# Attention 1: row loads over 48 data partitions, key rows of ones written once, products for maxima over 48 rows

## What is computed

```python
q = jnp.einsum('bld,dhe->blhe', x, Wq)
k = jnp.einsum('bld,dhe->blhe', x, Wk)
v = jnp.einsum('bld,dhe->blhe', x, Wv)
a = jnp.einsum('bqhd,bkhd->bhqk', q, k) / Dh ** 0.5
a = jnp.where(mask, a, NEG_INF)
a = jax.nn.softmax(a, axis=-1)
o = jnp.einsum('bhqk,bkhd->bqhd', a, v)
return jnp.einsum('blhe,hed->bld', o, Wout)
```

## Time and profile before

| | |
|---|---|
| median of 3 runs | 1116.33 us (1116.32 to 1117.96) |
| the profiled execution | 1120.27 us, its span 1118.5 us |
| attention 1's matmuls | from 476.8 us to about 821 us of the span |
| PE busy | 921.9 us (82%) |
| DVE busy | 781.9 us (70%) |
| ACT, POOL busy | 517.0 us (46%), 465.7 us (42%) |
| DMA queue 1 | 36189 packets, 45.41 MB, 13.5% of the 16 engines' time |
| granted clock of PE, mean of the span | 0.922 |

### The profile page before, as it was taken

The page is one execution under the profiler, slowest core; times in us unless marked ns, Lnnn a source line. Parts: engine busy times, 40 slices in busy tenths (PEclk is TensorE's granted clock), DMA queues, the critical chain, the costliest instruction groups (busy, mean ns, idle before and its releaser), DMA issues. The chain is left out here.

```text
span 1118.5 us, 18158 instructions
## 1 busy us (share of the span) xinstructions
PE 921.9 (82%) x6169; PEld 549.5 (49%) x6169; DVE 781.9 (70%) x1507; ACT 517.0 (46%) x755; POOL 465.7 (42%) x629
## 2 busy tenths in 40 slices
PE   6899999994476666457999888978839999999997
PEld 2445555552354444333444443434326776677765
DVE  6777777775688999367778786868545666666642
ACT  3666666785123334324767665756713122232221
POOL 3112222224345556612555564535434335453344
PEclk9999999998668889767999999989968999999999
DMA  9000000000000000343333332310000000000000
GB/s 287 18 10 10 9 9 9 9 0 20 9 20 9 9 26 10 86 123 104 98 91 90 95 101 82 94 71 5 12 1 11 20 7 12 19 19 19 9 1 19
DMA packets 36254, 46.25 MB, mean 41 GB/s; under 512 B 4134, under 2 KB 27174, under 8 KB 36190
## 3 DMA queue, kind: packets, MB, share of 16 engines
q1 hardware_dynamic: 36189, 45.41, 13.5%
HBM read 22.00 MB, written 15.27 MB: 33 GB/s over the span
## 5 line engine op out<-in xcount | busy, mean ns | idle before, releaser
L1553 ACT ACTIVATE PT<-PS 128x1024 f32<-128x1024 f32 x160 | 162.9, 1022 | 87.1 <-PE PS L1333 87.1
L1609 POOL TENSOR_SCALAR_AFFINE_SELECT PT<-PT 128x256 f32<-128x256 f32 (+1 forms) x224 | 95.0, 439 | 147.6 <-ACT PT L1553 146.5
L1948 POOL TENSOR_TENSOR PRE_sb<-PRE_sb,VA 128x512 f32<-128x512 f32 x64 | 82.2, 1284 | 146.8 <-DVE PRE_sb L1996 146.7
L1922 ACT ACTIVATE sg_d<-PS 128x512 f32<-128x512 f32 x64 | 38.2, 597 | 183.8 <-PE PS L1070 183.7
L1647 DVE TENSOR_REDUCE negm<-PS 128x2 f32<-128x1024 f32 x64 | 78.0, 1225 | 44.1 <-PE PS L1322 42.6
L356 ACT ACTIVATE E<-PS,m 128x512 f32<-128x512 f32 x128 | 86.2, 684 | 40.3 <-PE PS L281 25.5
L1996 DVE TENSOR_TENSOR PRE_sb<-sg_d,PS 128x512 f32<-128x512 f32 x64 | 43.5, 687 | 82.6 <-ACT sg_d L1922 81.3
L1348 PE MATMUL PS<-PT,VA 128*32 128x512 f32 (+3 forms) x1024 | 92.7, 459 | 3.3 <-POOL PT L1609 3.3
L1318 PE MATMUL PS<-kS,qS 51*128 51x384 bf16 (+3 forms) x512 | 75.9, 319 | 22.0 <-DVE spread L1750 8.6
L469 DVE TENSOR_SCALAR E<-E 128x512 f32<-128x512 f32 x128 | 68.6, 536 | 33.5 <-ACT E L356 29.7
L387 POOL TENSOR_SCALAR Qs<-Qs 128x1024 f32<-128x1024 f32 x32 | 35.0, 1096 | 116.2 <-ACT Qs L344 116.2
(11 more groups left out here) (269 smaller groups left out, 2130.1 us busy)
## 6 DMA issues: line engine op xcount, KB each, us to landing
qS<-qk_rows SPq DMA_DIRECT2D x32, 204.0 KB
kS<-qk_rows SPq DMA_DIRECT2D x32, 204.0 KB
qk_rows<-parts SPq DMA_DIRECT2D x32, 192.0 KB, 2.8
xs_sb<-XN_sb SPq DMA_DIRECT2D x23, 256.0 KB, 2.3
qk_rows<-parts SPq DMA_DIRECT2D x32, 128.0 KB, 2.8
X_sb<-in_x_dram SPq DMA_DIRECT2D x8, 256.0 KB, 6.8
gs<-PRE_sb SPq DMA_DIRECT2D x8, 256.0 KB, 2.3
qk_rows<-parts SPq DMA_DIRECT2D x32, 64.0 KB, 2.5
```

The costliest lines, as they stand in the source:

```text
L1553: nc.scalar.activation(PT[:, quad % 2, u, :], PS[:, b:b + 2, :].rearrange("p b n -> p (b n)"), ACT.Exp).then_inc(exp_ready, 1)
L1609: nc.gpsimd.affine_select(out=v, in_=v, pattern=[[0, 4 if u == 4 else 2], [1, P]], compare_op=ALU.is_ge, fill=0.0, base=0, channel_multipl ...
L1948: nc.gpsimd.tensor_tensor(acts[:, s, f, :], acts[:, s, f, :], W[:, slot, s, :], ALU.mult).then_inc(weighted, 1)
```

## The change

`qk_rows` has 48 rows in place of 51, and the row loads cover 48 partitions in place of 51. The ones of k's rows 48 to 50 no longer come with every load: `ones` is written into `kS`, for both slots and both `par`, by four DMAs in feed-forward 0 in place of the eight stores of `fixed` into DRAM. One memset on POOL goes. The products for maxima read 48 rows, the scores 51 as before.

```diff
-        self.fixed = sb("fixed", [3, 2, S], BF16)
+        self.ones = sb("ones", [3, S], BF16)
...
-        self.qk_rows = nc.dram_tensor("qk_rows", [2, 2, 2, 51, NPAIR * S], BF16, kind="Internal").ap()
+        self.qk_rows = nc.dram_tensor("qk_rows", [2, 2, 2, 6 * DH, NPAIR * S], BF16, kind="Internal").ap()
...
-            own, heads = slice(64 * par, 64 * par + 51), slice(4 * h, 4 * h + 4)
+            own, heads = slice(64 * par, 64 * par + 6 * DH), slice(4 * h, 4 * h + 4)
...
-            sp.wait_ge(cleared, 4)
+            sp.wait_ge(cleared, 3)
             for slot in range(2):
-                for m in range(2):
-                    for par in range(2):
-                        sp.dma_start(pr.qk_rows[slot, m, par, 48:51, :].rearrange("r (a s) -> r a s", a=NPAIR),
-                                     pr.fixed[:, m, :].unsqueeze(1).broadcast_to([3, NPAIR, S])).then_inc(fixed_out, 16)
+                for par in range(2):
+                    sp.dma_start(pr.kS[64 * par + 48:64 * par + 51, slot, :, :],
+                                 pr.ones[:, :].unsqueeze(1).broadcast_to([3, NPAIR, S])).then_inc(fixed_out, 16)
...
-            sp.wait_ge(fixed_out, 16 * 8)
+            sp.wait_ge(fixed_out, 16 * 4)
...
-            nc.gpsimd.memset(pr.fixed[:, 0, :], 0.0).then_inc(cleared, 1)
-            nc.gpsimd.memset(pr.fixed[:, 1, :], 1.0).then_inc(cleared, 1)
+            nc.gpsimd.memset(pr.ones[:, :], 1.0).then_inc(cleared, 1)
...
-            pool.wait_ge(cleared, 4)
+            pool.wait_ge(cleared, 3)
...
-            def operands(slot, quad, j):
-                own = slice(64 * (j % 2), 64 * (j % 2) + 51)
+            def operands(slot, quad, j, rows):
+                own = slice(64 * (j % 2), 64 * (j % 2) + rows)
...
-                        q, key = operands(slot, quad, j)
+                        q, key = operands(slot, quad, j, 48)
...
-                    q, key = operands(slot, quad, j)
+                    q, key = operands(slot, quad, j, 51)
```

## The result

The changed kernel takes 1089.64 us (median of 4 runs, 1087.02 to 1091.99) against 1116.32 us before (1116.18 to 1117.96): ratio 0.9742, 95% interval 0.9705 to 0.9778. The profiled execution took 1091.99 us, with a span of 1090.3.

A forecast was written before the change was run, and what follows sets the result against it. The prediction took PE to bound attention 1, held up by waits behind row loads of 51 partitions on three DMA engines. It summed -14.5 - 7.2 - 6 = -27.7 us off 1116.3, giving 1089 us, range 1082 to 1101.

The forecast's parts named there:

- Three engines with 51 partitions, sixteen with 48: Row loads in attention 1: DMA engines used are the largest number up to 16 dividing the partitions, 3 then 16.
- The loads' length: Four row loads ahead of an exchange of maxima: 4.5 us in place of 10.6.
- -14.5 us for the waits for the maxima: Attention 1: all seven waits of PE's scores matmuls for the load of the maxima go, 14.5 us.
- -7.2 us at the start: Start of attention 1: PE's wait for the staging of `xs`, issued behind eight row loads, goes, 7.2 us.
- -6 us for the clock: Attention 1: PE's time lost at the lower clock behind long stalls goes, 6 us, bounds 0 and -8.
- three stalls: Clock means from 530, 680 and 740 us: 12.2 us at the lower level behind stalls, half of it lost.
- Nothing given back: Attention 1 without the stalls: PE sets its own pace, so 0 us is given back, with 3 us as bound.
- DVE does not take over: Rival: PE's waits for DVE in attention 1 grow as its slack shrinks, 1099 or 1104 us; chance 0.08.
- Small edits: One POOL memset less, four DMAs for eight at feed-forward 0's end, matmuls over 48 rows: zero each.
- The issue of a row load: On SP: 0.30 us could become 0.61, sending the store of the maxima up to 1.2 us later, within 3 us slack.
- The lower end of the range, 1082 us: Whole kernel: the time with the clock at its bound and the first sequence faster too.
- The rivals that kept the loads slow: Row loads on as few engines: 1111 to 1116 us, chance 0.06; also costlier for SP to issue: 1124 us, chance 0.04.

The follow-up runs named there:

- the experiment at the start alone: Kernel before, with only the eight row loads of sequence 0 cut into 48 and 3 partitions, later loads keeping 51; 1111.51 us, ratio 0.9932.
- The stall that was put back: Kernel after, with only the row loads of half 0 of the last sequence cut into 17, 17 and 14 partitions; 1096.91 us, ratio 0.9806.
- the kernel with 48 and 3 partitions: Kernel before, with each row load cut into two DMAs of 48 and 3 partitions, fixed rows still loaded; 1087.94 us, ratio 0.9739.

## Why the prediction was right

The forecast was 1089 us, and 1089.64 was measured. By its steps:

- **Three engines with 51 partitions, sixteen with 48.** Right. The shares with 51, 52, 54, 57 and 17 partitions (0.19, 0.79, 0.57, 0.21, 0.06) and with 48 (full) are those of 3, 13, 9, 3, 1 and 16 engines, each the largest number up to 16 that divides the partitions. The Trainium skill states this rule ("DMA: Bandwidth & Descriptors", "Why a DMA increments its semaphore by 16 and not by 1"). These shares agree with it.
- **The loads' length.** I took 4.5 us for four loads, from the 175 GB/s of stores of 64 partitions; they took 4.8 us, at 167 GB/s from first packet to last. The estimate of 1.9 us came of the Trainium skill's rule for the engines (the same section) and of a rate that I let grow with them. The rule gives the engines, not the rate, and the rate did not grow so.
- **-14.5 us for the waits for the maxima.** Right: seven waits gone. But the working expected the store behind the loads still, with 3 to 8 us for the exchange; it takes 1.4 to 2.9. What I had not seen, and read from SP's timelines, is that the old exchange itself kept SP from issuing the next stores and loads in time. With a short one, the loads go out 7.5 us ahead of the store, and the slack is larger than I worked out.
- **-7.2 us at the start.** Right by PE's row at 479.24 and by the medians of the experiment at the start alone (-7.6 us, 4 to 11); that experiment's profile shows only 4.0 us of it at the end of attention 1, since its next stall grew.
- **-6 us for the clock.** The size came out, in part by luck: PE's busy time fell by 6.91 us for the same matmuls, but this is a gain of 9.03 us up to the last 54 matmul instructions and a loss of 2.13 in these. The rows before and after, split there:

```profile
476.77:810.57 333.80, 282.88 (x3451) 140.49 (x3453) 250.72 (x462) 204.45 (x247) 154.25 (x317) 0.92 0.28 81
810.57:829.43 18.86, 6.59 (x54) 3.55 (x54) 6.31 (x22) 2.69 (x5) 6.98 (x18) 0.74 0.01 1
```

```profile
475.08:779.48 304.40, 273.85 (x3451) 136.84 (x3453) 252.83 (x462) 204.42 (x247) 155.20 (x317) 0.96 0.37 84
779.48:800.49 21.01, 8.72 (x54) 4.53 (x54) 6.33 (x22) 2.69 (x5) 7.01 (x18) 0.60 0.00 1
```

  The clock stood at 1.00 from 520 us on, as forecast, but only to 780 us; then it fell, sooner than before. The working had counted three stalls and nothing at the end. Single executions also differ: PE's busy time was 289.1 to 294.6 us in the three profiles with the later loads of 51 partitions in the old order, and 280.4 to 284.0 in those with short loads throughout. The stall that was put back cost 1.74 us of clock at its place where I expected 3 to 4. Little comes of the start: with the start alone changed, PE's busy time was 289.07 us in place of 289.48.
- **Nothing given back.** Nearly: stalls of 21.7 us went, PE's idle time fell by 20.34. The other 1.4 us are short waits of several kinds, none of which grew by more than about 1 us; the largest, for DVE's maxima, rose by 0.4 us in the table of waits. DVE does not take over: it is busy 259.16 of 325.41 us, 80%.
- **Small edits.** Right for the products over 48 rows (1118.68 us). The issue of a row load rose from 0.30 to 0.42 us rather than to 0.61, inside the slack. The memset and the four writes of ones were not tried by themselves; the kernel with 48 and 3 partitions, which has neither edit, is as fast.

The sum was -27.7 us; attention 1 lost 27.25 us and the median 26.7. That the two agree within 0.5 us is closer than the terms are known. The lower end of the range, 1082 us, is not covered by the terms: with the clock at its bound of -8 they give 1086.6, and no row stands for the other 4.6 us. The rivals that kept the loads slow did not come in, since the rate rose and an issue took 0.42 us. The case nearest to them is the kernel with 57 partitions at 81 GB/s; its median issue time is 0.31 us, so its 1133.76 us come of the loads' length and not of their issue.

## What to carry to other kernels

Look at the share of DMA while one kind of DMA runs alone: a flat 3, 1 or 9 sixteenths says how many engines carry it, and a partition count with a better divisor, even a larger one, or a cut into two DMAs can mend it. It need not be all sixteen: here nine were enough. Weigh a transfer's length by what is queued behind it and by the queue that waits for it, not by whether its own data is late: here the rows themselves were in time, and a small exchange behind them was not. Moving the small DMA ahead of the long one can make it worse, if the long one has no slack of its own.

## What the runs showed of the hardware that I had not expected

- The rate grows less than the number of engines. In the middle of the row loads, with runs of 4 KB, it was 26 GB/s on one engine, 79 on three, 176 on nine, 213 on thirteen and 205 on sixteen: 26 GB/s an engine with one and three, 13 with sixteen. Over all four loads it was 76, 173, 185 and 167 GB/s with three, nine, thirteen and sixteen. Loads of 128 partitions reached 351 with a share of 0.98, so sixteen busy engines can move more than these loads did. No run shows what holds them.
- Where eight row loads follow one another, at the start of attention 1, the last two took 2.01 and 3.04 us each to issue with three engines, and 0.42 us each with sixteen; the last one there:

```profile
464.88 0.42 SPq L559 DMA_DIRECT2D kS<-qk_rows  x1
```

- The time to issue such a load on SP grows with the engines that it uses, but slowly: a median of 0.30 us with three, 0.32 with nine, 0.37 with thirteen and 0.42 with sixteen (loads of `kS`, of 51, 54, 52 and 48 partitions; the rows are below, in this order).

```profile
L559 SPq DMA_DIRECT2D kS<-qk_rows x32: 283/302/3043, 463.5 to 741.8; - x32
```

```profile
L559 SPq DMA_DIRECT2D kS<-qk_rows x32: 303/322/880, 461.5 to 713.5; - x32
```

```profile
L559 SPq DMA_DIRECT2D kS<-qk_rows x32: 358/372/1498, 460.8 to 712.8; - x32
```

```profile
L559 SPq DMA_DIRECT2D kS<-qk_rows x32: 409/423/1880, 462.1 to 714.3; - x32
```
